# A post-norm decoder layer on one core: a new order at the joint of its two attentions, four norms on ScalarE, and earlier unpacking of three feed-forward tiles

## What is computed

```python
x = layernorm(x + self_attention(x))          # 32 heads of 16, causal, bias; weights 512 x 512
x = layernorm(x + cross_attention(x, ctx))    # 32 query heads, 8 key/value heads of 128, rope on q and k
x = layernorm(x + ffn(x))                     # silu(x Wg) * (x Wu) Wd, 4-bit weights, inner size 1376

def layernorm(x):                             # over the last axis of 512
    return (x - mean(x)) / sqrt(var(x) + 1e-5)
```

## Time and profile before

| | us |
|---|---|
| median of 3 runs (lowest, highest) | 874.25 (873.38, 874.68) |
| the profiled execution, its own time | 875.49 |
| its span, first to last instruction | 873.6 |
| PE busy | 833.4 (95%) |
| DVE busy | 704.3 (81%) |
| POOL busy | 610.9 (70%) |
| ACT busy | 530.9 (61%) |

### The profile page before, as it was taken

The page is one execution under the profiler, slowest core; times in us unless marked ns, Lnnn a source line. Parts: engine busy times, 40 slices in busy tenths (PEclk is TensorE's granted clock), DMA queues, the critical chain, the costliest instruction groups (busy, mean ns, idle before and its releaser), DMA issues.

```text
span 873.6 us, 17358 instructions
## 1 busy us (share of the span) xinstructions
PE 833.4 (95%) x6125; PEld 469.2 (54%) x6125; DVE 704.3 (81%) x1094; ACT 530.9 (61%) x1555; POOL 610.9 (70%) x538
## 2 busy tenths in 40 slices
PE   8899999998899999999999999999999799999997
PEld 3567777555445555555555555555554544434444
DVE  5588898887867877879789788696889665799897
ACT  4788889454565666656675676666564662777400
POOL 0165959896657775777877677668688733799896
PEclk9999999999999999999999999999999899999999
DMA  6765244203135413324323214213412312231001
GB/s 173 232 200 181 75 134 155 77 1 122 26 91 127 110 37 86 84 50 133 94 59 121 61 38 134 60 25 86 91 38 79 91 37 67 78 105 60 2 37 60
DMA packets 120038, 76.76 MB, mean 88 GB/s; under 512 B 72877, under 2 KB 104336, under 8 KB 119952
## 3 DMA queue, kind: packets, MB, share of 16 engines
q1 hardware_dynamic: 117504, 74.86, 31.3%
q10 hardware_dynamic: 2448, 0.79, 0.4%
HBM read 52.50 MB, written 6.36 MB: 67 GB/s over the span
## 4 chain that ended last, share of the span: by engine, by line
PE 51%; POOL 18%; DVE 11%; ACT 9%; issue 7%; DMA 3%; SPq 0%; ACTq 0%; DVEq 0%; POOLq 0%
PE bank L354 14%; PE bank L355 14%; PE bank L356 14%; POOL rot L636 3%; ACT prob L972 2%; POOL left L669 2%; ACT prob L821 2%; POOL q2l L642 1%; POOL xqs L585 1%; DVE rsin L1209 1%; PE bank L1780 1%; PE bank L1781 1%; POOL xql L589 1%; PE bank L1699 1%; PE bank L1700 1%
## 5 line engine op out<-in xcount | busy, mean ns | idle before, releaser
L646 POOL TENSOR_TENSOR prob<-prob,rden 128x512 f32<-128x512 f32 x64 | 66.8, 1044 | 115.6 <-DVE rden L1267 115.3
L636 POOL TENSOR_TENSOR rot<-rcos,rsin 128x512 f32<-128x512 f32 x80 | 107.3, 1341 | 18.0 <-DVE rsin L1209 18.0
L354 PE MATMUL bank<-aTh,xqh 128*128 128x512 f16 x256 | 97.8, 382 | 3.5 <-DVE aTl L1099 2.5
L354 PE MATMUL bank<-xoh,o2h 128*128 128x512 f16 x256 | 97.0, 379 | 0.8 <-DVE o2l L1099 0.8
L355 PE MATMUL bank<-aTl,xqh 128*128 128x512 f16 x256 | 97.7, 382 | 0.0
L356 PE MATMUL bank<-aTh,xql 128*128 128x512 f16 x256 | 97.6, 381 | 0.0
L355 PE MATMUL bank<-xol,o2h 128*128 128x512 f16 x256 | 97.0, 379 | 0.0
L356 PE MATMUL bank<-xoh,o2l 128*128 128x512 f16 x256 | 97.0, 379 | 0.0
L972 ACT ACTIVATE prob<-bank,ebias 128x128 f32<-128x128 f32 x256 | 90.4, 365 | 2.1
L653 POOL TENSOR_TENSOR pn<-prob,pn 128x512 f16<-128x512 f32 x64 | 84.3, 1317 | 8.6 <-ACT pn L984 8.4
L1209 DVE SCALAR_TENSOR_TENSOR rsin<-bank,sinq 64x512 f32<-64x512 f32 x128 | 88.1, 688 | 1.7
(11 more groups left out here) (219 smaller groups left out, 2649.9 us busy)
## 6 DMA issues: line engine op xcount, KB each, us to landing
tst<-tables SPq DMA_DIRECT2D x11, 768.0 KB, 5.6
xqs<-in_xwq SPq DMA_DIRECT2D x8, 1024.0 KB, 7.1
xos<-in_xwo SPq DMA_DIRECT2D x8, 1024.0 KB, 5.6
qst<-in_fq SPq DMA_DIRECT2D x11, 384.0 KB, 3.4
kstk<-stack SPq DMA_DIRECT2D x48, 64.0 KB, 2.2
qstk<-stack SPq DMA_DIRECT2D x21, 128.0 KB, 2.6
xs<-in_ctxT SPq DMA_DIRECT2D x2, 1024.0 KB, 7.3
res<-in_x SPq DMA_DIRECT2D x1, 2048.0 KB, 8.3
```

The lines of the kernel that those rows point to most:

```text
L354: pe.matmul(out_ap, ah, bh, start=first, stop=False)
L636: nc.gpsimd.tensor_tensor(rot[:, r % 2, :], rcos[:, r % 2, :], rsin[:, r % 2, :], ALU.add).then_inc(rope_rot, 1)
L646: nc.gpsimd.tensor_tensor(prob[:, v % 2, :].rearrange("p (h k) -> p h k", h=QH), prob[:, v % 2, :].rearrange("p (h k) -> p h k", h=QH), rd ...
```

## The change

1. ACT: the casts of rotated fills (`rotations`) go from the start of a step to its end before `T0`, and behind `seed_mask` in step v = 0. POOL's `rotated_lo` follows one step later before `T0`.
2. The norms of batches 4 to 7 go from DVE to ACT (`scaled_norm`: res * rs + shift, one activation each); POOL computes the shift (`lnsh` = -mean * rs), a third small instruction behind its two.
3. DVE adds the `o` fills of steps 0 and 1 before `row_sum_inverse`; in steps 2 and 3 it takes `t`, `k` and `o_lo` in another order.
4. PE: the transpose of batch 4 goes ahead of the `k` fill in step 2; in step 3 merge(0) and the transpose of batch 7 go ahead of weigh(1). ACT makes `o_hi(0)` ahead of `exps(2)`.
5. Tiles 1, 2 and 3 are unpacked in steps 48, 49 and 53 instead of 50, 54 and 57 (the digits of tile 3 were made in 55); the casts of tile 1 go from step 51 to 50.

The diff, cut to its core:

```diff
-    plan += [(T0 + 2, "k", (2,)), (T0 + 2, "t", (0, 4)), (T0 + 2, "t", (0, 5)), (T0 + 3, "t", (0, 6)), (T0 + 3, "t", (0, 7))]
+    plan += [(T0 + 2, "t", (0, 4)), (T0 + 2, "k", (2,)), (T0 + 2, "t", (0, 5)), (T0 + 3, "t", (0, 6)), (T0 + 3, "t", (0, 7))]
...
-    return [f for f in fills_at(t)[:1] if FILLS[f][1] == "t"]
+    return [f for f in fills_at(t)[:2 if t == T0 + 3 else 1] if FILLS[f][1] == "t"]
...
+SHIFTED = [(0, b) for b in range(BH, NB)]
...
-CODES_SLOT = {0: T0 + 26, 1: T0 + 50, 2: T0 + 54, 3: T0 + 57, 4: T0 + 62, 5: END + 4}
-DIGITS_SLOT = {**CODES_SLOT, 3: T0 + 55}
-WEIGHTS_SLOT = {0: T0 + 34, 1: T0 + 51, 2: T0 + 56, 3: T0 + 61}
+CODES_SLOT = {0: T0 + 26, 1: T0 + 48, 2: T0 + 49, 3: T0 + 53, 4: T0 + 62, 5: END + 4}
+WEIGHTS_SLOT = {0: T0 + 34, 1: T0 + 50, 2: T0 + 56, 3: T0 + 61}
...
+                if divmod(e, NB) in SHIFTED:
+                    pool.wait_ge(ln_rs, e + 1)
+                    nc.gpsimd.tensor_scalar(lnsh[:, SHIFTED.index(divmod(e, NB)), :], lnmv[:, e % 3, 0:1], lnrs[:, e % 3, :], -1.0,
+                                            ALU.mult, ALU.mult).then_inc(ln_shift, 1)
...
+                if v in (0, 1):
+                    inverse_sd(BH + 2 * v)
                 if 0 <= v < STEPS:
                     p_norm(v)
+                if v in (0, 1):
+                    inverse_sd(BH + 2 * v + 1)
...
-                rotations(fills_at(t - 1))
                 if j + 1 < BLOCKS and n == 4 and t > -TILES1:
...
                 bank_splits([f for f in fills_at(t) if f not in turned_first(t)])
+                rotations(fills_at(t - 1))
+
+            def scaled_norm(layer, b):
+                e, r = layer * NB + b, res[:, b, :]
+                act.wait_ge(ln_shift, SHIFTED.index((layer, b)) + 1)
+                nc.scalar.activation(r, r, ACT.Identity, scale=lnrs[:, e % 3, :],
+                                     bias=lnsh[:, SHIFTED.index((layer, b)), :]).then_inc(ln_out, 1)
...
+                shifted = [(layer, b) for layer, b in SHIFTED if APPLY_SLOT[(layer, b)] == t]
+                for layer, b in shifted[:1]:
+                    scaled_norm(layer, b)
+                if v == 2:
+                    o_hi(0)
                 if v < STEPS:
                     exps(v)
+                for layer, b in shifted[1:]:
+                    scaled_norm(layer, b)
...
-                early = [f for f in fills_at(t)[:1] if f in ROPES] + turned_first(t)
+                early = [f for f in fills_at(t)[:1] if f in ROPES] + turned_first(t) + [f for f in fills_at(t) if FILLS[f][1] == "o"]
+                if v == 2:
+                    early += [find_fill("k", 2)]
...
-                for f in fills_at(t)[:1]:
+                first = 2 if v == 2 else 1
+                for f in fills_at(t)[:first]:
                     fill(f)
-                if v == STEPS + 1:
+                if v in (3, STEPS + 1):
                     merge(v - 3)
+                if v == 3:
+                    fill(find_fill("t", 0, 7))
```

More of the change, by code:

```diff
@@ L707, in inverse_sd @@
                 nc.gpsimd.tensor_tensor(lnrs[:, e % 3, :], lnve[:, e % 3, :], power[:, :], ALU.pow).then_inc(ln_rs, 1)
+                if divmod(e, NB) in SHIFTED:
+                    pool.wait_ge(ln_rs, e + 1)
+                    nc.gpsimd.tensor_scalar(lnsh[:, SHIFTED.index(divmod(e, NB)), :], lnmv[:, e % 3, 0:1], lnrs[:, e % 3, :], -1.0,
+                                            ALU.mult, ALU.mult).then_inc(ln_shift, 1)
             def inverse_sds(layer, t):
                 for (norm, b), slot in APPLY_SLOT.items():
-                    if norm == layer and slot == t + 1:
+                    if norm == layer and slot == t + 1 and (norm, b) not in SHIFTED:
                         inverse_sd(layer * NB + b)
@@ L726, in _ @@
                 inverse_sds(1, t)
-                for f in fills_at(t - 1)[:1]:
-                    if f in ROPES:
-                        rotated_lo(f)
+                if t < T0:
+                    for f in fills_at(t - 2):
+                        if f in ROPES:
+                            rotated_lo(f)
+                if v >= 1:
+                    for f in fills_at(t - 1)[:1]:
+                        if f in ROPES:
+                            rotated_lo(f)
+                if v in (0, 1):
+                    inverse_sd(BH + 2 * v)
                 if 0 <= v < STEPS:
                     p_norm(v)
-                for f in fills_at(t - 1)[1:]:
+                if v in (0, 1):
+                    inverse_sd(BH + 2 * v + 1)
+                for f in fills_at(t - 1)[1 if v >= 1 else 0:] if v >= 0 else []:
                     if f in ROPES:
@@ L1254, in apply_norms @@
                 for (layer, b), slot in APPLY_SLOT.items():
-                    if slot == t:
+                    if slot == t and (layer, b) not in SHIFTED:
                         normalised(layer, b)
@@ L1433, in _ @@
                         consume(f)
[L1434 removed]
+                if 2 < v <= STEPS + 1:
                     o_lo(v - 2)
                 for f in fills_at(t)[1:]:
[L1437 removed]
+                    if f not in early:
+                        consume(f)
                 if t in LATE_TURN:
@@ L1873, in _ @@
                     weigh(v - 2)
-                rest = fills_at(t)[1:]
+                rest = fills_at(t)[first:] if v != 3 else []
                 behind = rest[1:] if v >= 3 and len(rest) == 2 else []
@@ L1877, in _ @@
                     fill(f)
-                if 3 <= v <= STEPS + 2 and v != STEPS + 1:
+                if 3 < v <= STEPS + 2 and v != STEPS + 1:
                     merge(v - 3)
```

30 lines of the change are left out of this document (20 added, 10 removed).

## The result

| | us |
|---|---|
| before, median of 4 runs (lowest, highest) | 874.46 (873.38, 874.71) |
| with the change, median of 4 runs | 859.01 (858.55, 860.29) |
| ratio, 95% interval | 0.9828 (0.9810 to 0.9846) |
| the profiled execution with the change, its own time | 858.55 |
| its span | 856.7 |

The change takes 15.45 us off the time, 1.7%. The forecast was 860.0 in a range of 856 to 869, faster with 0.90.

The account below looks back on a forecast made before the run. PE was taken as the bound, busy 833.4 of 873.6 us. Terms 3.4 + 1.0 + 1.4 + 1.9 + 1.7 + 5.8 = 15.2, less 1.0, took 875.49 to 861.3, median forecast 860.0; range 856 to 869.

Parts of the forecast that it names:

- casts last: Joint of the two attentions, before scores(0): PE's waits of 1.19, 1.63 and 0.54 us all go, 3.4 us.
- sums: Steps 0 and 1 at the joint: with DVE's sums ahead of the reciprocal, PE's 0.98 us wait goes, 1.0 us.
- norms: First steps of the second attention: norms on ACT and moved transposes turn PE's 2.98 us wait into a 1.4 us gain.
- the 2.12: PE's wait at 246.34 us for aTl of the last transpose: about 0.2 us stays, 1.9 us goes.
- the clock: Joint, 243.4 to 250.6 us: with no wait of that size left, PE's clock no longer falls and 1.7 us comes back.
- moved tiles where they go: Steps 48 and 49: extra unpacking work on DVE and POOL fits in 2.9 us of slack, costed at nothing.
- late: End of the second attention: 5.0 us wait for v2l goes, 2.0 clock returns, 1.2 new wait for pT: together 5.8.
- set aside for margins that don't hold: Whole sum: 1.0 us taken off because many in-order waits in the walk have margins of only half a microsecond.
- three new waits: Joint: PE newly waits 0.4 us for k-fill rotation parts, 0.3 for pT of tile 0, 0.9 at batch 7's transpose.
- The ring at the joint: First steps of the second attention bound by scores-to-exponentials round; third to fifth terms give nothing, clock falls: 865.0 us, chance 0.16.
- The stall in steps 48 to 52: DVE and POOL stretch each other's long instructions; PE waits 3.5 us, plus 1.7 with a clock fall: 865.2 us, chance 0.14.
- The slower rival: Joint: weigh(0) late by a 7.7 us transfer, steps 2 to 5 each pay a full latency round: 882 us, chance 0.06.

Follow-up runs that it names:

- Run 3: The kernel before with only ACT's casts of rotated fills last in the step and POOL's rotated_lo a step later before T0: 868.56 us, 0.9939.
- run 7: The change with DVE's sums of the o fills back behind the reciprocal in steps 0 and 1: 861.92 us, 0.9860.
- run 12: The change with ACT's cast of the transpose of batch 5 right behind exps(2), tile 3's slots untouched: 858.60 us, 0.9825.
- run 4: The change with the norms of batches 4 to 7 back on DVE: 860.48 us, 0.9843.
- run 6: The change with PE's old order in step 3, merge(0) and the transpose of batch 7 behind weigh(1): 861.97 us, 0.9856.
- Run 5: The kernel before with POOL's scaling of tile 3 moved behind the product of tile 58 and its rotation: 877.51 us, 1.0027.
- run 11: The change, unaltered, measured again on the chip of a later group of runs: 858.96 us, 0.9823.
- run 2: The kernel before with only the change's earlier unpacking slots for tiles 1 to 3: 869.66 us, 0.9944.
- run 1: The change with tiles 1 to 3 unpacked in the old slots, steps 50, 54 and 57: 864.63 us, 0.9889.
- runs 8 and 10: The change with tiles 1, 2, 3 in steps 46, 50, 54: 859.61 us; with tile 3 in step 54 and batch 5's cast earlier on ACT: 859.00 us.

## Why the prediction was right, term by term

The forecast of the time missed by 1.0 us, and for each stretch the trace can be held against its term.

| term | predicted | measured |
|---|---|---|
| casts last, to scores(0) | 3.4 | 4.3 |
| sums, norms, the 2.12, the clock: 1.0 + 1.4 + 1.9 + 1.7 | 6.0 | 6.3 |
| moved tiles where they go | 0 | -0.7 |
| late: 5.0 + 2.0 - 1.2 | 5.8 | 5.7 |
| set aside for margins that don't hold | -1.0 | |
| sum | 14.2 | 15.6 |

*Casts last.* The mechanism was right, the size too small by 0.9. Two things were left out. The change also took a wait of PE for `prob` of 0.83 us further ahead, and gave back 0.35 for `res` in the same place:

```profile
161.66 0.66 PE L1607 MATMUL bank<-ident,prob 128*128 128x128 f32 x4 [0.83 <-ACT prob L821]
```

(the kernel before). And a wait costs more than the idle time printed beside it. In an unbroken stream a matmul of 512 columns takes 0.38 but the next starts 0.22 after it, so 0.16 lie on top of each other. In front of these three waits stand matmuls of 17 columns, which take 0.17 and follow each other after 0.02 to 0.03, so 0.15 overlap. Behind a wait this overlap is missing. Three waits of 3.36 in all, 3 x 0.15, and 0.83 - 0.35 make 4.3. This is a reckoning from rows; no run tried it alone.

*Sums before the reciprocal.* Here the step failed, though the size looks right. I gave the 0.98 wait to the order of the sums. Run 3 shows that ACT's late cast was enough to make it: with the cast last, `dens` of tile 0 comes in time and the sums may stay where they were. The prediction even named that cast as the cause of the late `dens`, and then priced the remedy that wasn't needed. What the order of the sums does buy, 1.9 us, lies a step later, behind the reciprocal of tile 1, and comes from other parts of the change: `inverse_sd` ahead of the product of tile 0 on POOL, and a norm ahead of the exponentials of tile 1 on ACT (run 7). Of that place the prediction said that the maximum of tile 1 would be ready no sooner than ACT. The timelines of DVE and ACT in the changed kernel say otherwise:

```profile
219.53 0.66 DVE L1296 TENSOR_REDUCE nmax<-bank 128x4 f32<-128x512 f32 x1
```

```profile
220.77 0.62 ACT L1005 CAST pn<-prob 128x512 f16<-128x512 f32 x1 [2.56 <-POOL prob L648]
221.29 0.81 ACT L982 ACTIVATE res<-res,lnsh,lnrs 128x512 f32<-128x512 f32 x1
222.01 0.19 ACT L787 ACTIVATE ebias<-nmax 128x4 f32<-128x4 f32 x1
```

The maximum is there at 220.2, the exponentials start at 222.2. It cost PE nothing, since the sums no longer stand behind them.

*Norms on ACT and the three new waits.* I expected 0.4 for the rotation parts, 0.3 for `pT` of tile 0, and 0.9 at the transpose of batch 7, and found none, 0.15 and 0.81. The third was named with its cause, the cast of batch 5 behind `exps(2)`, and run 12 confirms it: with this cast ahead that wait goes, though 0.74 of it, with the 0.19 behind, comes up again one fill later. The size of each edit was then seen alone: run 4 gives the norms 1.8 us, run 6 gives PE's order 4.4 us in the trace (37.66 against 33.22, a fall of the clock in it) and 3.0 in the medians. A norm on ACT takes 0.80, the mean of four, not the 0.70 taken from the earlier trace rows:

```profile
L982 ACT ACTIVATE res<-res,lnsh,lnrs 128x512 f32<-128x512 f32 x4 | 3.2, 804 | 0.0
```

The row of before had one operand by pointer, this one has two. The Trainium skill, ScalarE: Activation LUTs, in its section on what ACT_TABLE_LOAD costs, gives a fixed part to each such operand; by its figures an estimate for 512 columns with two is 0.80, and the trace agrees.

*The 2.12 and the clock.* Both as predicted: 0.19 stays, and no stretch at the lower clock is left at the joint. The two are not independent, as the sum had them: in run 3 the clock fell ahead of this wait, and its price then lay inside it. That the joint's total came out at 6.3 for 6.0 is partly luck: the sums were priced for the wrong wait (1.0, and they bought 1.9), and of the 1.8 of waits that were to be left or new (0.4 + 0.3 + 0.9 + 0.2) 1.15 came. The second group of projections starts at 236.08, 10.3 us sooner and not 8; 1.3 of it is the first two rows of the table of stretches, 0.9 the first term.

*Late.* Each piece came out: 5.08 to 0.21, a new wait of 1.09 for `pT` of tile 60 where 1.2 was said, the clock whole. Run 5 confirms the head of the chain, and that one step of distance is not enough.

*Moved tiles.* The step "I cost this at nothing" failed by some 0.7 us. It was argued for steps 48 and 49 and holds there. The cost is around tile 3, whose new place I had not walked: 0.31 and 0.50 in the first profile, a single wait of 0.99 for `rsin` at the query fill of 638.68 in that of run 11. The seven profiles with the new slots have 92.92 to 93.08 us for steps 47 to 59. Of those with the old ones, before has 92.32 (against 92.92 in run 2, which differs in nothing else) and run 1 has 92.09 (against 93.06 with the change): 0.6 and 1.0. But run 3, with the old slots too, has 92.92, so the cost of the move is not fixed better than 0 to 1.0. The two other choices tried, runs 8 and 10, don't get it back.

*The 1.0 set aside* was for small waits that my walk had not seen. There was one, the 0.7 above, so the discount was about right; that the forecast still fell 1 us short is mostly the 0.9 of the first term. The forecast's own range doesn't follow from its bounds, though: the lower ones (1.7, 1.0, 3.3 and three times nothing) sum to 6.0, which gives 868.2 and not 865.

*The rivals.* The ring at the joint would have left stalls in scores(0) to scores(5); they sum to 1.15. The stall in steps 48 to 52 didn't come. Its mechanism did. The timelines of POOL and DVE in step 48 of the changed kernel:

```profile
590.10 1.47 POOL L644 TENSOR_TENSOR k2l<-rot,k2h 128x512 f16<-128x512 f32 x1
591.53 1.99 POOL L638 TENSOR_TENSOR rot<-rcos,rsin 128x512 f32<-128x512 f32 x1
593.47 1.16 POOL L655 TENSOR_TENSOR pn<-prob,pn 128x512 f16<-128x512 f32 x1
```

```profile
417.56 0.96 DVE L1355 TENSOR_TENSOR dif<-nib,tst 128x1536 f16<-128x1536 uint16 x1
...
589.51 1.04 DVE L1340 TENSOR_SCALAR nib<-qst,shq 128x1536 uint16<-128x1536 uint16 x1
590.59 1.79 DVE L1355 TENSOR_TENSOR dif<-nib,tst 128x1536 f16<-128x1536 uint16 x1
```

`dif` takes 0.96 where POOL stands idle and 1.79 here; `k2l` and `rot` take 1.47 and 1.99 where their shortest are 1.15 and 1.26. From the start of `k2l` to the end of `rot` it is 3.42 us, and the three alone would make 0.96 + 1.15 + 1.26 = 3.4, as if they ran one after another. The Trainium skill, SBUF — State Buffer, in its part on reading the diagram, has the rule that a DVE instruction with two SBUF inputs and a GpSimd instruction that reads SBUF hold a shared port pair in turn, each for the whole instruction. The trace agrees to 0.1 us; it is one case, and the last 0.45 of `nib` lies in the same stretch, so the count is not exact. What the rival got wrong is the price to PE: the transfer of tile 48 had 2.9 us of slack, and PE was busy for 10.00 of 10 us. The slower rival needed late transfers at the joint; the longest wait for one was 0.15. Its sum also mixes two figures: a round of 7 in place of 4 costs 3 a step, and the 4.7 that it multiplies is a transfer of 7.7 less the 3.0 of the median.

## What to carry to other kernels

An in-order engine that waits for a slow partner should do so last in its step: moving one cast of 0.62 us behind the work that others wait for was worth between a third and a half of this change, and it removed waits that the trace had put down to DVE. When two remedies meet one wait, try each alone before pricing both: the order of the sums got credit for a wait that the cast had made, and earned its own 1.9 us elsewhere. A wait that shrinks in a new profile is not yet a gain: compare the time between two instructions on either side of it, since the engine may only have been slower ahead of it. Work that sits at the head of a chain must be moved far enough; one step away it cost 2.6 us here and gave the wait another name.

## What the runs showed of the hardware that was not expected

*The same wait does and does not bring the clock down.* Near 30 us every version has a wait of PE for `prob` and little work around it. The timelines of PE in two profiled executions of the changed kernel, the first one and run 11:

```profile
30.35 0.66 PE L1648 MATMUL bank<-ident,prob 128*128 128x128 f32 x4 [2.56 <-ACT prob L836]
```

```profile
29.96 1.12 PE L1648 MATMUL bank<-ident,prob 128*128 128x128 f32 x4 [2.57 <-ACT prob L836]
```

The wait is the same to 0.01 us; in the second the transpose behind it takes 1.12 instead of 0.66. The windows of 20 to 40 us of the first and of run 11:

```profile
20.00:40.00 20.00, 15.45 (x152) 10.39 (x151) 10.04 (x17) 13.41 (x42) 3.53 (x4) 1.00 0.69 209
```

```profile
20.00:40.00 20.00, 15.89 (x149) 11.28 (x148) 10.04 (x17) 13.50 (x41) 3.53 (x4) 0.91 0.71 213
```

The Trainium skill, TensorE: Matmul & The Clock Gate, in its section on what's actually happening, says of the rise at a kernel's start that its moment varies from run to run. These two differ in whether the clock falls at all, behind a wait in the middle of the work. Ten of the thirteen profiles that were read show 0.91 between 20 and 40 us, with waits near 30 us from 1.43 to 3.13, and three show 1.00, with 2.04, 2.56 and 2.58; in runs 5 and 12 the clock was at its lower level already at 24 to 27 us. No clear price of it shows: the first 31 tiles take 74.4 to 75.8 us with the fall and 74.0 to 75.1 without.

*At the joint* the clock fell behind a wait of 2.12 (before), 2.66 (run 3) and 1.95 with 0.85 (run 6), and not behind 1.71 with 0.67 (run 4). Before, it stayed whole behind the 2.98, through 6.3 us of PE's work at full clock, and fell 0.6 us after the 2.12; in run 3 it fell 1.2 us after the 2.66. So a prediction that leaves one wait of some 2 us in place keeps the clock's loss as a case of its own; in run 6 it made more than half of the loss in the profiled execution (4.4 us, of which the waits had grown by 1.8; the rest is put down to the clock by subtraction).
